# W2 first on the queue, three casts ahead of the gelu layer, and weights stored by rank: a small network's prelude to a long recurrence

## The reference

```python
ae = layernorm(cond) * ln_g + ln_b
h = gelu(ae @ w1 + b1)                   # 2 x 256
x_a, x_b = split(h @ w2 + b2)            # w2: 256 x 4096, both halves reshaped to (2, 256, 8)
layer = base + einsum('bdr,bkr->bdk', x_a, x_b)
x = x + (x + x @ layer)
h_t = tanh(h_{t-1} @ Wh + x_t @ Wx + b)  # 1,024 steps, h_0 = cond
out = x + h_t
```

## Time and profile before

| | us |
|---|---|
| median of three runs | 768.34 |
| the profiled execution | 767.74 |
| its span in the trace | 764.9 |
| outside the span | 2.8 |
| prelude: start of the span to the first product of the recurrence | 30.25 |
| granted TensorE clock | 1.00 |

### The profile page before, as it was taken

How to read it: one execution, slowest core, us unless ns; L and a number is a source line. 1 busy time by engine, 2 the same in 40 slices (tenths; PEclk the granted TensorE clock), 3 DMA queues, 4 the chain that set the end, 5 groups by cost and what they waited for, 6 DMA issues and landing times.

```text
span 764.9 us, 45957 instructions
## 1 busy us (share of the span) xinstructions
PE 689.3 (90%) x18801; PEld 623.6 (82%) x18801; DVE 283.4 (37%) x1539; ACT 497.8 (65%) x5140; POOL 6.4 (1%) x18
## 2 busy tenths in 40 slices
PE   5699999999999999999999999999999999999997
PEld 5588888888888888888888888888888888888886
DVE  6533333333333333333333333333333333333332
ACT  6466666666666666666666666666666666666665
POOL 3000000000000000000000000000000000000000
DMA  8000000000000000000000000000000000000000
GB/s 279 10 6 10 11 11 9 11 7 9 11 11 8 11 8 9 11 11 9 10 7 9 11 11 9 11 7 9 11 11 9 11 8 7 11 11 9 7 7 6
DMA packets 12285, 12.36 MB, mean 16 GB/s; under 512 B 1813, under 2 KB 11056, under 8 KB 12080
## 3 DMA queue, kind: packets, MB, share of 16 engines
q1 hardware_dynamic: 11984, 9.45, 4.3%
q0 software_dynamic: 96, 0.02, 0.0%
HBM read 7.36 MB, written 2.10 MB: 12 GB/s over the span
## 4 chain that ended last, share of the span: by engine, by line
PE 76%; ACT 19%; issue 2%; DMA 1%; SPq 1%; DVE 1%; DVEq 0%; another core or an unknown queue 0%
PE acc L320 49%; ACT h_pre L446 19%; PE pre L320 14%; PE p_w L284 4%; PE pre L300 4%; PE p_w L279 2%; DMA x_in<-x_dram 1%; PE p_w L274 1%; PE pre L297 1%; SPq L218 1%; PE pre L401 0%; SPq L215 0%; DVE lay_s L687 0%; DVE lay_f L683 0%; DVE ab_t L676 0%
## 5 line engine op out<-in xcount | busy, mean ns | idle before, releaser
L320 PE MATMUL acc<-h_pre,wh_s 128*128 128x2 f16 x8192 | 385.5, 168 | 57.8 <-DVE acc L562 0.6
L446 ACT ACTIVATE h_pre<-pre 128x2 f16<-128x2 f32 x2046 | 240.7, 170 | 251.1 <-PE pre L320 251.1
L320 PEld LDWEIGHTS acc<-h_pre,wh_s 128*128 128x128 f16 x8192 | 302.2, 106 | 121.1 <-ACT h_pre L446 105.0
L567 DVE TENSOR_TENSOR h_lo<-p_f,h_pre 128x4 f16<-128x4 f32 x1024 | 165.5, 162 | 461.7 <-ACT p_f L452 457.1
L320 PE MATMUL pre<-h_rnd,wh_s 128*128 128x2 f16 x4092 | 270.2, 170 | 0.0
L320 PE MATMUL acc<-h_lo,wh_s 128*128 128x2 f16 x4096 | 257.5, 167 | 0.0
L320 PEld LDWEIGHTS pre<-h_rnd,wh_s 128*128 128x128 f16 x4092 | 190.7, 108 | 0.1
L320 PEld LDWEIGHTS acc<-h_lo,wh_s 128*128 128x128 f16 x4096 | 189.2, 106 | 0.1
L456 ACT ACTIVATE h_f<-acc 128x4 f32<-128x4 f32 x1024 | 186.4, 182 | 0.5 <-PE acc L320 0.5
L454 ACT ACTIVATE h_rnd<-acc 128x4 f16<-128x4 f32 x1022 | 172.7, 169 | 0.0
L452 ACT ACTIVATE p_f<-acc 128x4 f32<-128x4 f32 x1023 | 161.6, 158 | 0.1
(11 more groups left out here) (76 smaller groups left out, 139.4 us busy)
## 6 DMA issues: line engine op xcount, KB each, us to landing
w_f<-w_dram SPq DMA_DIRECT2D x8, 512.0 KB, 8.4
x_in<-x_dram SPq DMA_DIRECT2D x32, 64.0 KB, 2.3
out_dram<-o_row SPq DMA_DIRECT2D x64, 32.0 KB, 1.9
w_f<-w_dram SPq DMA_DIRECT2D x1, 256.0 KB, 2.8
base_f<-base_dram SPq DMA_DIRECT2D x1, 256.0 KB, 10.8
wh_f<-wh_dram SPq DMA_DIRECT2D x1, 256.0 KB, 10.5
wx_f<-wx_dram SPq DMA_DIRECT2D x1, 256.0 KB, 10.5
cond_r<-cond_dram SPq DMA_DIRECT2D x1, 2.0 KB
```

The source lines that it names most:

```text
L320: return nc.tensor.matmul(dst, wh_s[:, pw, ki, mo * P:(mo + 1) * P], h[:, par, ki, :], start=False, stop=True, skip_group_check=True)
L446: nc.scalar.activation(h_pre[:, n % 2, m, :], src, func, scale=scale).then_inc(s_hpre[(n // HALF) % 2], 1)
L567: nc.vector.tensor_sub(h_lo[:, par].rearrange("p m b -> p (m b)"), p_f[:, 0:COLS], h_pre[:, par].rearrange("p m b -> p (m b)")).then_inc(s ...
```

## The change

1. SP issues the first piece of W2, then W1, the second piece, the first block of x, and the other six pieces; base, Wh and Wx follow. The condition and the three vectors are issued by ACT, ahead of its first activation.
2. ACT casts the first three pieces (`AHEAD = 3`) before gelu, and DVE subtracts them before L639. The other five follow gelu and L639.
3. The float16 parts of W2 are stored rank by rank. The weights of one rank are contiguous for PE. ACT's cast and DVE's subtraction now read the float32 piece with `by_rank`, a step of 8 numbers (32 bytes), and write contiguously; before, both read and wrote contiguously.
4. DVE's low part of x (L525) moves from ahead of L660 to behind the last L672.

```diff
-        w2_s = sb("w2_s", [P, 2, NM, 2 * D * RANK], F16)
+        w2_s = sb("w2_s", [P, 2, NM, 4, RANK, P], F16)
...
+        AHEAD = 3
+
+        def by_rank(ap):
+            return ap.rearrange("p (d r) -> p r d", r=RANK)
...
-            sync.dma_start(cond_r[:, :], cond).then_inc(s_cond, 16)
-            for n, v in enumerate((ln_g, ln_b, b1)):
-                sync.dma_start(vec_r[n * NM:(n + 1) * NM, :], v.rearrange("(m p) -> m p", p=P)).then_inc(s_vec, 16)
+            def load_w2(n):
+                q, k = W2_PIECES[n]
+                sync.dma_start(w2_f[:, k, tile_of_ab(q)], w2[k * P:(k + 1) * P, tile_of_ab(q)]).then_inc(s_w2[n], 16)
+
+            load_w2(0)
             sync.dma_start(w1_f[:, :, :], w1.rearrange("(k p) n -> p k n", p=P)).then_inc(s_w1, 16)
-            for n, (q, k) in enumerate(W2_PIECES):
-                sync.dma_start(w2_f[:, k, tile_of_ab(q)], w2[k * P:(k + 1) * P, tile_of_ab(q)]).then_inc(s_w2[n], 16)
+            load_w2(1)
+            sync.dma_start(x_in[:, :], x_rows[0:BLOCK]).then_inc(s_xload, 16)
+            for n in range(2, len(W2_PIECES)):
+                load_w2(n)
             sync.dma_start(base_f[:, :, :], base.rearrange("(k p) n -> p k n", p=P)).then_inc(s_base, 16)
-
-
-            sync.dma_start(x_in[:, :], x_rows[0:BLOCK]).then_inc(s_xload, 16)
...
+                for r in range(RANK):
+                    c = 64 + (q * RANK + r) * 2 * NB
+                    product = nc.tensor.matmul(pre[B][:, 0, c:c + 2 * NB], w2_s[:, pw, k, q, r, :],
...
+            act.dma_start(cond_r[:, :], cond).then_inc(s_cond, 16)
+            for n, v in enumerate((ln_g, ln_b, b1)):
+                act.dma_start(vec_r[n * NM:(n + 1) * NM, :], v.rearrange("(m p) -> m p", p=P)).then_inc(s_vec, 16)
             act.wait_ge(s_var, 1)
...
+            def w2_high(n):
+                q, k = W2_PIECES[n]
+                act.wait_ge(s_w2[n], 16)
+                nc.scalar.copy(w2_s[:, 0, k, q], by_rank(w2_f[:, k, tile_of_ab(q)])).then_inc(s_w2hi, 1)
+
+            for n in range(AHEAD):
+                w2_high(n)
             act.wait_ge(s_hmm, 1)
...
+            for n in range(AHEAD, len(W2_PIECES)):
+                w2_high(n)
...
+            def w2_low(n):
+                q, k = W2_PIECES[n]
+                dve.wait_ge(s_w2hi, n + 1)
+                nc.vector.tensor_sub(w2_s[:, 1, k, q], by_rank(w2_f[:, k, tile_of_ab(q)]),
+                                     w2_s[:, 0, k, q]).then_inc(s_w2lo, 1)
+
+            for n in range(AHEAD):
+                w2_low(n)
             dve.wait_ge(s_hidhi, 1)
...
+            for n in range(AHEAD, len(W2_PIECES)):
+                w2_low(n)
             keep_x()
             split_x_high()
-            split_x_low()
...
             last.then_inc(s_abst, 1)
+            split_x_low()
             low(wh_s, wh_f, 0)
```

More of the change, by code:

```diff
@@ L392, in _, with w2_products @@
             pe.wait_ge(s_hid, 1)
-            for n, (q, k) in enumerate(W2_PIECES):
+            def w2_products(n, pw):
+                q, k = W2_PIECES[n]
+                for r in range(RANK):
+                    c = 64 + (q * RANK + r) * 2 * NB
+                    product = nc.tensor.matmul(pre[B][:, 0, c:c + 2 * NB], w2_s[:, pw, k, q, r, :],
+                                               hid_s[:, k].rearrange("p s b -> p (s b)"),
+                                               start=n == 0 and pw == 0 and r == 0, stop=True, skip_group_check=True)
+                return product
+            for n in range(len(W2_PIECES)):
                 if n == 6:
                     turn_x()
[L396 to L403, removed]
+                pe.wait_ge(s_w2hi, n + 1)
+                w2_products(n, 0)
+                pe.wait_ge(s_w2lo, n + 1)
+                last = w2_products(n, 1)
             last.then_inc(s_abcol, 1)
@@ L488, in high @@
                                      scale=SCALE).then_inc(s_hi, 1)
-            for n, (q, k) in enumerate(W2_PIECES):
-                act.wait_ge(s_w2[n], 16)
-                nc.scalar.copy(w2_s[:, 0, k, tile_of_ab(q)], w2_f[:, k, tile_of_ab(q)]).then_inc(s_w2hi, 1)
+            for n in range(AHEAD, len(W2_PIECES)):
+                w2_high(n)
             high(wh_s, wh_f, s_wh)
@@ L673, in _, with low @@
             last.then_inc(s_abst, 1)
+            def low(dst, src, n):
+                dve.wait_ge(s_hi, n + 1)
+                nc.vector.scalar_tensor_tensor(
+                    dst[:, 1].rearrange("p k n -> p (k n)"), src[:, :, :].rearrange("p k n -> p (k n)"), SCALE,
+                    dst[:, 0].rearrange("p k n -> p (k n)"), ALU.mult, ALU.subtract).then_inc(s_split, 1)
+            split_x_low()
             low(wh_s, wh_f, 0)
```

## The result

The changed kernel takes 771.84 us (median of six runs, 771.33 to 772.16), against 768.37 us before. The ratio is 1.0047, 95% interval 1.0034 to 1.0060: slower, where 766.7 us was forecast. The profiled execution takes 771.85 us with a span of 769.9. The span grew by 5.0 us and the execution by 4.1; the part outside the span was 0.9 us shorter this time. The medians differ by only 3.5 us, because the profiled execution of before was one of its quicker ones: its span of 764.9 us stands beside median spans of 765.3 to 765.9 in the later executions of that kernel.

A forecast was written before the change was run, and what follows sets the result against it. Prelude bound by transfers up to 19.47 us, then PE's backlog. Gains of 0.96 (earlier last subtraction) and 0.72 (PE weights) less 0.08 (x's low part) make 1.60 us: 766.7 us forecast, range 766.0 to 774.8.

The forecast's parts named there:

- the price of the strided reads for ACT and DVE: W2 casts and subtractions in the prelude: reading float32 with a 32-byte step was taken to cost nothing.
- the smaller bound: Upper bound for strided W2 reads: 0.47 ns more per number, cast 1.53 us, subtraction 1.71 us.
- The larger bound: Upper bound for strided W2 reads from the ratio of PE's steps, about two: cast 1.88 us, subtraction 2.30 us.
- The shift of 1.07 us: W2 transfers in the prelude: last piece lands earlier by 1.30 less 0.23 us for x's block; 0.68 kept as lower bound.
- rival B: Prelude transfers do not move as said: 767.1 us, or 767.6 if small loads hold up the first piece; chance 0.14.
- the slow stretch: Transfers from 4.5 to 9 us, at 279 GB/s against 398 from 9 to 17; it coincides with POOL's work.
- Rival C: Strided reads slow casts and subtractions, deciding from about 0.25 ns per number: 770.2 us, or 774.6 if doubled; chance 0.25.
- its doubled form: Strided reads double cast and subtraction times in the prelude: ab_sum at 26.9, 6.3 us lost, 774.6 us; chance 0.17.
- The small transfers on ACT: Four small loads issued by ACT before its first activation: warm activation ends at 5.03 in place of 4.68, hidden.
- Gelu behind the third cast: Prelude: PE starts at 12.2 in place of 9.21 with 48 products waiting, and has caught up by 14.0.
- Weights by rank for PE: After the last subtraction only 8 products remain: ab_sum follows by 0.52 us in place of 1.24, a gain of 0.72.
- x's low part: DVE's low part of x, moved from ahead of ab_sum to the wait for PE's transposes, costs 0.08 us.

The follow-up runs named there:

- the order alone: The changed kernel with W2's float16 parts stored as before, so ACT and DVE read contiguously and PE every eighth column; 768.10 us, ratio 1.0004.
- the best kernel: The changed kernel with W2 stored as before, two casts ahead of gelu, and b2 loaded after GpSimd's other transfers; 765.44 us, ratio 0.9974.
- the run with two casts: The changed kernel with W2 stored as before and two casts ahead of gelu in place of three; 766.88 us, ratio 0.9984.

## Why the prediction was wrong

**The step that failed** is the price of the strided reads for ACT and DVE: "this is why I take nothing: the store gives separate places at 0.48 ns, and DVE asks at 1.05". A rate at which one engine takes separate places said nothing about another. Each cast lost 1.00 us (0.98 ns per number), each subtraction 0.80 us (0.78 ns). Both are above the smaller bound of 0.47 ns. The larger bound, the doubling, holds DVE's subtraction (2.30 expected, 2.02 measured), but ACT's cast lies beyond it (1.88 expected, 2.05 measured).

In the forecast's own terms, the last subtraction was to end at 18.51 and ended at 25.07. With the order alone it ended at 19.64. So 5.4 of these 6.6 us are the reads and 1.1 us are the next step.

**The shift of 1.07 us** is the second step that failed. The last cast starts at 17.33 in the kernel with the order alone, against 17.17 to 18.12 with the old order. The sum priced x at its own 0.23 us and no more; together with b2's load it costs more. Moving b2 brought the last cast forward by 1.6 us with three casts ahead and by 1.7 with two, moving x by 1.3 and by 0.7. With b2 out of the way the shift is there: the last cast starts at 15.77 and 15.70, at least 1.40 us earlier than in the three traces of the old order. So rival B's condition, that the transfers do not move as said, held as well. Its argument that the slow stretch belongs to what GpSimd does is refuted for b2's load only.

**Rival C**, given 0.25, was the case, in its doubled form for ACT. Its time of 774.6 is 2.8 us too high. Half of that is at ab_sum, 26.9 against 25.61: five subtractions at 1.96 us from one to the next make 9.8 us, not 11.5, though they began 0.4 later. The other half, some 1.4 us, is the starting point. Every time of the prediction was built as the median before plus a difference from one quick execution, and the median grew by less than that trace's span did. From where on the step decides ("about 0.25 ns") no run shows; none has a cost between nothing and 0.78 ns.

**The small transfers on ACT**: the warm activation ended at 5.19 (5.03 forecast). The vectors landed late, and PE turned them at 5.70 in place of 3.03; no step of the prediction had that. It is hidden as said, because gelu stands behind casts anyway. In the best kernel, with two casts ahead, ACT waits 0.34 us for PE before gelu, but its later casts wait for transfers again, so the last one is not later for it.

**Gelu behind the third cast** was priced as 48 waiting products that PE works off by 14.0. At the contiguous weights' step that holds: 56 products took 1.66 us. PE began at 15.39 in place of 12.2, behind the slow casts. With the old storage it costs 1.0 us at ab_sum, as the run with two casts shows.

**Weights by rank for PE**: right. The 8 products behind the last subtraction took 0.37 us, and ab_sum came 0.54 us after it (0.52 forecast). With the reads at their price, it is a gain of 0.7 us for a loss of over 5.

**x's low part** was to cost 0.08 us; the trace shows 0.00.

## What to carry to other kernels

A layout that makes one engine's reads contiguous moves the step to whoever writes it. Price that side first, in time per number at the step in bytes, and on the engine that would do it: here 60 ns on each of a piece's 16 weight loads were bought with 1.0 us of ACT and 0.8 us of DVE per piece. A bound that decides the sign of the forecast deserves the caution of its worst row, not an argument from another engine's rate; here even the worst row was passed. A trace is one execution: before a landing time is compared, see how far it varies in the same kernel. And when large transfers are brought forward, look at which small ones then run beside them.

## What the runs showed of the hardware

- ACT's cast and DVE's subtraction read float32 without loss up to a step of 8 bytes (1.08 and 1.22 us for 1,024 numbers) and take about 1.9 ns per number from 16 bytes on (1.85 to 2.02 us at 16 to 64 bytes).
- A DVE copy to float16 loses less by a 32-byte step (0.68 to 1.06 us) than a subtraction (1.23 to 1.98).
- Writing float16 with a step of 256 bytes is dearer: 4.73 us on ACT and 2.43 us in a DVE copy, against 1.04 and 0.68.
- Two small transfers, 64 KB in 512-byte rows and 16 KB in 32-byte runs, together took the rate of all to 179 to 194 GB/s for two microseconds (four traces); with either one elsewhere it was 246 to 301 (five traces).
- GpSimd's scaling of b_row (256 numbers) takes 0.86 us when no subtraction of DVE runs, 1.64 us beside a contiguous one, and 2.56 us beside a strided one. In both cases it ends 0.7 us after the end of that subtraction (8.90 after 8.19, 9.86 after 9.19), so what counts is how long the subtraction lasts.
